# A wide gather behind a sweep: one core, four graph layers, GpSimd's queue re-ordered

## The reference, cut to what matters

```
h = relu(layernorm(x));  x = x + SGConv(relu(SGConv(h)))         # layer 0: two sums over edges
h = relu(layernorm(x));  x = x + relu(W1(h + segment_sum(relu(h[src] + edge_attr), dst)))
h = relu(layernorm(x));  x = x + 8 steps of attention-weighted segment sums
h = relu(layernorm(x));  x = x + 10 steps of degree-normalised segment sums
```

## Time and profile before

| | us |
|---|---|
| median of 3 runs | 9387.37 (9373.32 to 9389.24) |
| profiled execution, its own time | 9330.52 |
| its span in the trace | 9328.4 |
| POOL busy | 5707.4 (61%) |
| DVE busy | 5625.3 (60%) |
| PE busy | 1645.2 (18%) |
| ACT busy | 591.1 (6%) |

### The profile page before, as it was taken

One profiled execution on the slowest core, in us unless ns is written; L12 is line 12 of the kernel. 1 busy time (PEld: TensorE's weight loads), 2 busy tenths in 40 slices (PEclk: granted clock), 3 DMA queues, 4 the chain that ended last, 5 costly groups with the idle time before them and its releaser, 6 DMA issues.

```text
span 9328.4 us, 62184 instructions
## 1 busy us (share of the span) xinstructions
PE 1645.2 (18%) x7434; PEld 1182.6 (13%) x7434; DVE 5625.3 (60%) x18903; ACT 591.1 (6%) x1241; POOL 5707.4 (61%) x5754
## 2 busy tenths in 40 slices
PE   3554424211344200451002200000000000000000
PEld 1123323211233200341002200000000000000000
DVE  4557856658887724345768878855556765444520
ACT  0001111100111100110000000000000000000000
POOL 4767767546766675655757247076652376677777
PEclk8655555555555555555555555555555555555555
DMA  7014323211344562343344421124333122433220
GB/s 234 0 32 93 93 47 83 66 30 27 84 117 114 127 196 70 82 117 81 101 111 108 116 47 49 42 47 41 41 34 59 53 47 57 42 44 40 35 26 19
DMA packets 1189999, 664.52 MB, mean 71 GB/s; under 512 B 1046539, under 2 KB 1059776, under 8 KB 1189924
## 3 DMA queue, kind: packets, MB, share of 16 engines
q10 hardware_dynamic: 880608, 373.78, 14.7%
q0 software_dynamic: 174880, 156.46, 12.5%
q1 hardware_dynamic: 134436, 133.62, 4.8%
HBM read 236.69 MB, written 430.16 MB: 71 GB/s over the span
## 4 chain that ended last, share of the span: by engine, by line
POOL 34%; DVE 28%; issue 25%; DMA 4%; another core or an unknown queue 3%; PE 3%; POOLq 1%; DVEq 1%; SPq 1%; ACT 1%; ACTq 0%
POOL G L555 15%; POOL look L555 6%; POOL pair L555 4%; POOL seatmap L559 4%; DVE G L2001 4%; DVE st L1494 3%; POOL out L559 3%; DVE xm L1507 2%; PE TR L1197 1%; DVE G L1991 1%; DVE xm L1520 1%; SPq L419 1%; PE HP L1189 1%; PE TR L1207 1%
## 5 line engine op out<-in xcount | busy, mean ns | idle before, releaser
L555 POOL DMA_INDIRECT G<-tab,idxs x1260 | 1339.2, 1063 | 452.3 <-issue 405.2
L555 POOL DMA_INDIRECT look<-flagtab,idxs x588 | 619.8, 1054 | 205.9 <-issue 177.3
L555 POOL DMA_INDIRECT X<-in_x,dst_gat x392 | 422.4, 1077 | 201.5 <-issue 120.3
L555 POOL DMA_INDIRECT G<-alt_e,idxs x420 | 440.1, 1048 | 151.1 <-issue 136.2
L1197 PE MATMUL TR<-w4T,shared 128*128 128x64 f32 x2356 | 490.4, 403 | 224.7 <-ACT shared L960 168.4
L1197 PEld LDWEIGHTS TR<-w4T,shared 128*128 128x128 f32 x2356 | 476.9, 313 | 317.4 <-issue 317.4
L555 POOL DMA_INDIRECT pair<-lookup,idxs x392 | 424.4, 1083 | 139.5 <-issue 120.6
L555 POOL DMA_INDIRECT G<-alt_d,idxs x392 | 404.0, 1031 | 138.8 <-issue 125.0
L559 POOL DMA_INDIRECT seatmap<-vals,idxs x392 | 399.5, 1019 | 140.7 <-issue 126.8
L1494 DVE BATCH_NORM_STATS2 st<-xin 128x6 f32<-128x64 f32 x3136 | 420.7, 211 | 56.9 <-DVE rowsC L1511 16.6
L1214 PE MATMUL HP<-ident,tcar 128*64 128x128 f32 (+1 forms) x21 | 8.7, 415 | 2388.6 <-DVEq L1419 1733.0
(11 more groups left out here) (540 smaller groups left out, 7233.1 us busy)
## 6 DMA issues: line engine op xcount, KB each, us to landing
tab<-rowsB ACTq DMA_DIRECT2D x98, 448.0 KB, 2.5
tab<-rowsC ACTq DMA_DIRECT2D x98, 448.0 KB
xin<-tab SPq DMA_DIRECT2D x84, 448.0 KB
raw<-G ACTq DMA_DIRECT2D x84, 448.0 KB
tab<-rowsA ACTq DMA_DIRECT2D x70, 448.0 KB
tab<-rowsE ACTq DMA_DIRECT2D x70, 448.0 KB, 2.5
tab<-spare ACTq DMA_DIRECT2D x2, 12544.0 KB
xin<-in_x SPq DMA_DIRECT2D x56, 448.0 KB
```

The source lines that it names most:

```text
L555: pool.indirect_dma_start(to, None, table, bass.IndirectOffsetOnAxis(ap=index, axis=0), bounds_check=bound, oob_is_err=False).then_inc(s, 16)
```

## The change

Three edits and the buffers that they need.

**Buffers.** rowsA, rowsC, rowsE, spare and rowsD become parts of one block, `wide_block`, and two halves of that block are the wide gather's tiles, seven columns each (WIDE = 7, before 5).

**POOL's order.** The wide gather leaves its place ahead of the edge rows. Ahead of sweep A the edge rows are chunks 8 to 21 (14 chunks, before 10). Behind sweep A's own 252 gathers `stage_rows` runs: for each of the ten late chunks two halves of seven wide gathers, each half waiting until the store of that half's previous content is done. The edge rows of chunks 18 to 21 that stood there are gone from there; those of 22 to 27 stay behind sweep B.

**SP's order.** In sweep A's late part SP stores the two halves of chunk 18 + m, loads the chunk's own rows, waits for both stores and for `staged_ready` of that chunk, and loads the staged rows back.

**Zero fills.** ACT also waits for `map_init` before its four fills.

A second form of the late rows (`refill`, taken when a chain is longer than the early columns) is rearranged too; it isn't executed with these inputs.

```diff
-        HEAD, MID, EDGES = 5, 8, 5
-        TAIL = [4, 6]
+        HEAD, MID, EDGES = 5, 8, 7
+        TAIL = [6]
...
-        WIDE = 5
-        wide_rows = [t.rearrange("p (j f) -> p j f", j=WIDE)
-                     for t in (shared[:, 0:WIDE * NK * D], shared[:, SL:SL + WIDE * NK * D],
-                               xin[:, :, :, :].rearrange("p s j f -> p (s j f)")[:, 0:WIDE * NK * D])]
+        WIDE = HALF_CH
+        wide_rows = [wide_block[:, n * WIDE * NK * D:(n + 1) * WIDE * NK * D].rearrange("p (j f) -> p j f", j=WIDE)
+                     for n in (0, 1)]
...
-            for g in range(DEAD // WIDE):
-                slot, part = g % len(wide_rows), g // len(wide_rows)
-                sp.wait_ge(staged_some[slot], 16 * WIDE * (part + 1))
-                sp.dma_start(staged[:, g * WIDE:(g + 1) * WIDE, :], wide_rows[slot]).then_inc(staged_stored[slot], 16)
...
+                if k == "a":
+                    for m in range(K3):
+                        for h in (0, 1):
+                            sp.wait_ge(staged_some[h], 16 * WIDE * (m + 1))
+                            at = m * CH + h * WIDE
+                            sp.dma_start(staged[:, at:at + WIDE, :], wide_rows[h]).then_inc(staged_stored[h], 16)
+                        load_own(SPLIT + m, m % 2)
+                        for h in (0, 1):
+                            sp.wait_ge(staged_stored[h], FIRST + 16 * (m + 1))
+                        sp.wait_ge(staged_ready, m + 1)
+                        load_staged(k, m, m % 2)
...
-            last_row(whole)
-            for j in range(DEAD):
-                slot, part = j // WIDE % len(wide_rows), j // WIDE // len(wide_rows)
-                if j % WIDE == 0 and part:
-                    pool.wait_ge(staged_stored[slot], 16 * part)
-                gather(wide_rows[slot][:, j % WIDE, :], whole, idxD[:, j:j + 1], staged_some[slot])
...
+            def stage_rows():
+
+                many = pool.value_load(againI[0:1, 1:2], min_val=0, max_val=1)
+                for m in range(K3):
+                    last_row(whole)
+                    for h in (0, 1):
+                        pool.wait_ge(staged_stored[h], r_wide[h].reg)
+                        pool.sem_inc(pool_waited, 1)
+                        r_wide[h].skip(16)
+                        for j in range(WIDE):
+                            at = m * CH + h * WIDE + j
+                            gather(wide_rows[h][:, j, :], whole, idxD[:, at:at + 1], staged_some[h])
...
+                    pool.sem_inc(staged_ready, 1)
...
             sweep("a")
-            tail_rows(TAIL0, TAIL[0])
+            stage_rows()
...
             act.wait_ge(zeros_ready, 1)
+            act.wait_ge(map_init, 16)
```

More of the change, by code:

```diff
@@ L158, in _build, with part_of @@
         lnw = sb("lnw", [P, 6, CH])
-        rowsA = sb("rowsA", [P, CH, D])
+        wide_block = sb("wide_block", [P, 4 * CH * D + CH * AW])
+        def part_of(at, w):
+            return wide_block[:, at:at + CH * w].rearrange("p (j f) -> p j f", f=w)
+        rowsA, rowsC, rowsE, spare = (part_of(n * CH * D, D) for n in range(4))
+        rowsD = part_of(4 * CH * D, AW)
         rowsB = sb("rowsB", [P, CH, D])
-        rowsC = sb("rowsC", [P, CH, D])
-        rowsD = sb("rowsD", [P, CH, AW])
-        rowsE = sb("rowsE", [P, CH, D])
         hT = sb("hT", [P, CH // 2, P])
@@ L170, in _build @@
         FR = sb("FR", [P, 2, AW])
-        spare = sb("spare", [P, CH, D])
         tcar = sb("tcar", [P, AW])
@@ L307, in _build @@
         dead_gathered = sem("dead_gathered")
-        staged_some = [sem(f"staged_some{n}") for n in range(3)]
-        staged_stored = [sem(f"staged_stored{n}") for n in range(3)]
+        staged_some = [sem("staged_some0"), sem("staged_some1")]
+        staged_stored = [sem("staged_stored0"), sem("staged_stored1")]
         staged_ready = sem("staged_ready")
@@ L383, in _build @@
         whole = tab[0:NK * N, :].rearrange("(n k) f -> n (k f)", k=NK)
-        WIDE = 5
-        wide_rows = [t.rearrange("p (j f) -> p j f", j=WIDE)
-                     for t in (shared[:, 0:WIDE * NK * D], shared[:, SL:SL + WIDE * NK * D],
-                               xin[:, :, :, :].rearrange("p s j f -> p (s j f)")[:, 0:WIDE * NK * D])]
-        assert WIDE * NK * D <= SL and DEAD % WIDE == 0
+        WIDE = HALF_CH
+        wide_rows = [wide_block[:, n * WIDE * NK * D:(n + 1) * WIDE * NK * D].rearrange("p (j f) -> p j f", j=WIDE)
+                     for n in (0, 1)]
         def staged_rows(k, c):
@@ L511, in _ @@
                         r_raw[s].skip(16)
[L512 to L516, removed]
+                if k == "a":
[9 more added lines that the diff above has]
+                        load_staged(k, m, m % 2)
+                else:
+                    sp.wait_ge(staged_ready, K3 + n)
+                    with sp.Fori(0, K3 // 2) as i:
+                        for s in (0, 1):
+                            load_own(2 * i + (SPLIT + s), s)
+                            load_staged(k, 2 * i + s, s)
             for s in (0, 1):
@@ L519, in _ @@
                 r_raw[s].skip(16 * (SPLIT // 2))
-            sp.wait_ge(staged_ready, 4)
+            sp.wait_ge(staged_ready, K3 + 3)
             with sp.Fori(0, K3 // 2) as i:
@@ L705, in _ @@
             pool.wait_ge(seats_cleared, 64)
-            last_row(whole)
-            for j in range(DEAD):
-                slot, part = j // WIDE % len(wide_rows), j // WIDE // len(wide_rows)
-                if j % WIDE == 0 and part:
-                    pool.wait_ge(staged_stored[slot], 16 * part)
-                gather(wide_rows[slot][:, j % WIDE, :], whole, idxD[:, j:j + 1], staged_some[slot])
-            for n in range(len(wide_rows)):
-                pool.wait_ge(staged_stored[n], 16 * len(range(n, DEAD // WIDE, len(wide_rows))))
             r_es2 = [Reached(pool, f"pool_edges{s}") for s in (0, 1)]
@@ L737, in _, with refill, refill_all @@
             r_ref = Reached(pool, "pool_refilled")
-            def refill(k):
+            def refill(k, c):
+                pool.tensor_copy(idxs[:, 0, :], idxA[:, ds(c * CH + EARLY, CH)]).then_inc(pool_step, 1)
+                pool.wait_ge(pool_step, r_step.more(1))
+                pool.sem_inc(pool_waited, 1)
+                last_row(tab)
+                for j in range(CH):
+                    gather(spare[:, j, :], tab, idxs[:, 0, j:j + 1], refilled)
+                pool.wait_ge(refilled, r_ref.more(16 * CH))
+                pool.sem_inc(pool_waited, 1)
+                pool.dma_start(staged_rows(k, c), spare[:, :, :]).then_inc(refilled, 16)
+                pool.wait_ge(refilled, r_ref.more(16))
+                pool.sem_inc(pool_waited, 1)
+            def refill_all(k):
                 many = pool.value_load(againI[0:1, 1:2], min_val=0, max_val=1)
@@ L743, in refill @@
                     with pool.Fori(0, K3) as c:
-                        pool.tensor_copy(idxs[:, 0, :], idxA[:, ds(c * CH + EARLY, CH)]).then_inc(pool_step, 1)
-                        pool.wait_ge(pool_step, r_step.more(1))
-                        pool.sem_inc(pool_waited, 1)
[L747 to L755, removed]
+                        refill(k, c)
+                pool.sem_inc(staged_ready, 1)
+            r_wide = [Reached(pool, f"pool_wide{h}", FIRST) for h in (0, 1)]
+            def stage_rows():
[4 more added lines that the diff above has]
+                        pool.wait_ge(staged_stored[h], r_wide[h].reg)
+                        pool.sem_inc(pool_waited, 1)
+                        r_wide[h].skip(16)
+                        for j in range(WIDE):
+                            at = m * CH + h * WIDE + j
+                            gather(wide_rows[h][:, j, :], whole, idxD[:, at:at + 1], staged_some[h])
+                    with pool.If(many > 0):
+                        for h in (0, 1):
+                            pool.wait_ge(staged_stored[h], r_wide[h].reg)
+                            pool.sem_inc(pool_waited, 1)
+                        refill("a", m)
+                    pool.sem_inc(staged_ready, 1)
             tails = [0, 0]
@@ L772, in sweep @@
             def sweep(k):
-                refill(k)
+                if k != "a":
+                    refill_all(k)
                 with pool.Fori(0, SPLIT // 2) as i:
@@ L847, in _ @@
             sweep("b")
-            tail_rows(TAIL0 + TAIL[0], TAIL[1])
+            tail_rows(TAIL0, TAIL[0])
             front_sums(raw, F_SEAT, F_TSEAT, D)
@@ L982, in _ @@
                 act.sem_inc(raw_stored[s], FIRST)
+                act.sem_inc(staged_stored[s], FIRST)
                 act.sem_inc(out_stored[s], FIRST)
```

## The result

Four runs of the changed kernel took 9222.97 us in the median (9214.41 to 9242.64), against 9380.35 (9309.09 to 9389.24) in four of the kernel before: a ratio of 0.9868, 95% interval 0.9819 to 0.9916. All ratios here are estimated from the fast runs of both kernels and are not quotients of the medians (here 0.9832). The profiled executions differ by 115.8 us (spans 9212.6 and 9328.4), and this is the difference that the traces can explain.

A forecast was written before the change was run, and what follows sets the result against it. No engine was busy over 61% of the span, so the chain of waits through POOL's indirect DMAs, in relay with DVE, was taken as the bound. From the median, 9387 with −64 − 95 + 67 = −92 gave 9295 us, range 9200 to 9372.

The forecast's parts named there:

- the second rival: Before sweep A: DVE's gaps go with the wide rows, gain there 160 us, kernel at 9230; chance 0.13.
- Part 1: Kernel start: zero fills behind `map_init` let POOL start near 20 us, −75, less +11 for slower scatters; net −64 us.
- The fill's price under the scatters: Seat scatters at the start: fill beside them costs 0.13 us per us; 88 us more overlap adds 11 us.
- Part 2: Ahead of sweep A: wide gathers leave, four more edge chunks come; sweep starts earlier, −95 us, between 56 and 160.
- nearer the first: Ahead of sweep A: −95 chosen nearer the 56 us gain, where DVE's gaps last as long as POOL gathers.
- the two rivals about the gaps: Ahead of sweep A: DVE's gaps follow POOL's gathers (9334, chance 0.20), or go with the wide rows (9230, chance 0.13).
- the port rule: DVE's loop before sweep A: VectorE and GpSimd share ports and block each other; alone it implies the 56 us gain.
- Part 3: Sweep A's end: ten times 14 wide gathers now stand there, end at 10P + 25; +67 us, bounds +36 and +117.
- P: Sweep A's end: pace of one staged chunk, 22 us forecast; 18.9 by POOL alone, 27 as upper bound.
- Staging as the bound: Sweep A's late part: stores and gathers alternate, break-even at pace 31, at 35 the kernel is 9425; chance 0.09.
- The fill did not take the start back: Rival at the start: fill costing 0.43 us per us makes the start's gain zero, kernel at 9359; chance 0.09.
- no change: Whole kernel: DVE paces the relay after the start, −56 and +67 cancel, 9398 at most; chance 0.07.

The follow-up runs named there:

- e1: Kernel before with one line of the change, the four zero fills also waiting for `map_init`; 9298.58 us, ratio 0.9985 (0.9945 to 1.0025).
- e6: Kernel before with the 140 wide gathers fetching 64 f32 of a row and not 320; 9552.54 us, ratio 1.0022 (0.9980 to 1.0065).
- e5: Kernel before with POOL waiting after each group of five wide gathers until they have landed; 9531.90 us, ratio 0.9969 (0.9932 to 1.0006).
- e2: Changed kernel without the zero fills' wait for `map_init`; 9234.14 us, ratio 0.9935 (0.9907 to 0.9963).
- e7: Changed kernel with POOL waiting ahead of the first wide gather until chunk 16's rows are stored; 9407.59 us, ratio 0.9865 (0.9806 to 0.9924).
- e10: Same program as e7, the changed kernel with POOL's wait at the turn of sweep A, on another chip; 9351.23 us, ratio 0.9781 (0.9710 to 0.9852).
- e9: Changed kernel as it is, a control on the chip of e10; 9362.28 us, ratio 0.9796 (0.9737 to 0.9856).

## Why the prediction was right, and where its steps were not

The time, 9222.97 against 9295 with 9200 to 9372, and the direction came out. The time lies 72 us under the forecast, though, and nearest to the second rival's 9230. The prediction's 0.2% as what a measurement can tell was too fine: the intervals here reach 0.3 to 0.7% to either side. The steps, by the two traces:

- **Part 1, −64 forecast, −47 measured.** The size was off in one term: the three loads were given 0.26 us each and took 18.9 together without the fill, and the map's landing 10.9 and not 6.44. I had taken the issue of a plain store for loads of another shape. The fill's price under the scatters was near: 17 us lost in all, 22.7 forecast. In e1, where this part stands alone, 36 us of it are left in the trace when the sweep starts, and the time can't tell it from nothing.
- **Part 2, −95 forecast, −153 measured.** The POOL sum was right (14 edge chunks in 281.8 us, 20.1 each). The step that failed is the choice "nearer the first" bound: the gaps' running on through the edge rows was read as a sign that they follow POOL's gathers as such. What the runs show: they came in all three traces in which the loop ran beside the 140 unbroken gathers (before, e1, and e6 with narrow rows), and were gone in the one with a pause of some 2 us after every five (e5). Beside edge gathers, where POOL stops for its index copy and for the one 2.2 us, they came and went: 0 to 3 us in sum in two traces (the changed kernel, e2), 9 to 12 in three, 50 to 100 in four. Of the two rivals about the gaps the second had the size (−160). As far as it means the rows' width, e5 and e6 refute its cause; but when the 140 unbroken gathers moved behind the sweep, the long gaps ahead of it did go. The first had the right engine and the wrong condition. That the changed kernel's trace has no gaps at all is partly chance; but DVE is done there 72 us ahead of POOL's last edge rows, so that smaller gaps would have cost nothing.
- From the port rule of the Trainium skill ("SBUF — State Buffer", "Who interferes with whom") the prediction drew that the gaps would last as long as POOL gathers. In e5 POOL gathered through the whole loop and there were none. The trace doesn't agree with it as the cause.
- **Part 3, +67 forecast, +75 measured.** P was 23 and not 22, and for another reason. The prediction put the surplus over POOL's 18.9 down to DMA engines that don't pack; in the changed kernel it was the turn: DVE stood for 69 us, SP stood behind DVE (44.7 us of waiting ahead of the own rows' loads) and the stores behind SP, 41.6 us of POOL's waiting. Where the turn was taken away (e7, and e10 on the chip of e9, whose P was 23) P was 20.0, and the DMA engines' share in e10's staged chunks was 0.94:

```profile
3973.00:4173.00 200.00, 94.85 (x378) 73.26 (x374) 65.84 (x173) 28.69 (x52) 145.11 (x140) 0.52 0.94 300
```

  At a share of 0.94 that is 18.8 us of all 16 engines per chunk, 6% under the 20.0 that part 3 had worked out from bytes and rates, and they packed better than the 0.9 assumed, which no row had shown.
- **The rest**: +10 in sweep B and behind, not forecast, of the size by which these stretches differ between any two traces here.
- Staging as the bound (the slower rival) did not come: P stayed under its 31. The fill did not take the start back, and "no change" fell with DVE's wait of 70.7 us for POOL at the lookups (84.9 before).

The sum −47 − 153 + 75 + 10 gives the −115 of the traces; −64 − 95 + 67 gave −92. Two errors of 17 and 58 had opposite signs, so the sum is nearer than its second term: that is luck. The medians differ by 157 us, 42 more than the profiled executions, and no trace here explains these 42.

What stays open is why VectorE's and TensorE's signals come late beside POOL's gathers. In the loop ahead of the sweep VectorE waits for its own signal, and its instructions' durations don't change; at the turn PE's matmuls are recorded as done 53 us before their signal arrives. No landing stands at a fixed distance from that moment: the last gather's data were in 0.5 us ahead of it in the changed kernel and 3 us in e9. Whether the pause or the landed data behind it sets the engines free was not told apart either, since each pause put in here was a wait for landing or for a store. Every run here carries the profiler's span and clock, so whether the recording itself has a part in it can't be told.

## What to carry to other kernels

A long run of indirect DMAs without a pause can hold up engines that share nothing with it in the program; look at the spacing of another engine's loop beside it, and at waits of an engine for its own signal. A wait for landing after every few gathers is a cheap test of it; here it took the gaps away (e5), but saved no time that could be measured. Where two lanes meet, a gain in one counts only down to the other's end: in e5 VectorE was done 230 us ahead of `tab<-fown`, and no difference in time could be told. Bytes over the rates of the trace gave the pace of the staging to within some per cent; the waits around it, which no row of before showed, made the difference.

## What the runs showed of the hardware

- Beside 140 indirect gathers issued 1.35 us apart VectorE's chunk took up to 37 us and not 7.5 in three traces (25.7 on average in the 13 chunks with gaps of the kernel before), whether a row had 1280 or 256 bytes; with a pause of some 2.3 us after every five (one trace) it took 7.5.
- In those chunks VectorE's instructions kept their 207 to 229 ns; a signal that it gives itself came up to 9.6 us late.
- At the turn of the sweep VectorE waited 49 to 72 us for TensorE's signal in six traces with unbroken wide gathers, and 9 to 13 in four in which POOL waited there. In two of the six the wait ended while POOL kept issuing.
- The same kernel took 9280 us in the median on one chip and 9573 on another, and between 9244 and 9394 in 26 runs on one.
